# Transposes of k and x1 moved from TensorE to VectorE block transposes and SP transfers

## The chip, the cores and the metric

The kernel runs on one core of a Trainium2 chip. The metric is the device time of one execution in microseconds. A core has TensorE (matrix products and transposes through an identity matrix), VectorE and ScalarE (elementwise work, both read PSUM), GpSimd (POOL) and SyncE (SP), which here only issues DMA transfers. Every engine works through its own queue in order; semaphores order the engines among each other.

## The reference

Two layers on 4096 tokens (8 sequences of 512) with 256 features, all in float32:

```
q1, k1 = rotary(x @ Wq), rotary(x @ Wk)        # 4 heads of 64
v      = x @ Wv                                # 4 heads of 128
o      = chunked retention(q1 / 8, k1, v)      # per head: decayed causal scores and a state S (64 x 128)
o      = rmsnorm(o, gn_weight) * silu(x @ Wg)
x1     = layernorm(x + o @ Wo)
h      = silu(x1 @ w_gate.T / 127) * (x1 @ w_up.T / 127)     # 768 wide, integer weights
out    = layernorm(x1 + h @ w_down.T / 127)
```

## The kernel before

The tokens are cut into 32 tiles (NT) of 128 rows. The kernel is a software pipeline in which slot s works on several tiles at once: the projections of tile s, the scores and the state of tile s - 1, the output of the heads of tile s - 2, the product with Wo of tile s - 3, and the FFN of tiles further back. Most products are made of two or three passes over float32 operands split into a high part (fp32r) and a remainder, so that each operand exists as a "hi" and a "lo" tile. Each engine's order of work is written out by hand, in one block of code for each engine; slots 9 (PACKED) to 31 follow `packed_slot`, and a `drain` follows them. The state is kept in halves of 64 rows from tile 8 (CHUNKED) on.

TensorE's packed slot is, in order: `down` (tile s - 7), the gate and up products of block s - 1 (parts 0 and 1, b_ffn), `turn_y` of tile s - 3, `keys_and_queries` (k of tile s, and queries already turned), part 2 of the block, `attention_out` of tile s - 3, `heads` (recall, scores of tile s - 1, state update, output of tile s - 2), `project` for v and g (L545), `turn_x1` (L711) and `turn_qk` (L558). The last product of `attention_out` (L527, b_rows<-wo,yT) carries the waits of `heads_ready`, so the queue stands still there until everything that `heads` reads is in place. `keys_and_queries`, `attention_out`, `down` and the gate and up products all run through the helper line L527 and are told apart by their tiles.

How k gets to the scores: VectorE multiplies k by cosines and sines (`packed_rotate_k`, L1574, L1577) and adds them in `sum_k` (L1531), which writes qk[:, s % 2, 256:512] and raises `rotated`. TensorE's `turn_qk` at the end of the slot transposes the two 128x128 blocks into PSUM (b_turn) and raises `qkT_done`. ScalarE's `keep_qk` (L1097) copies them to qkT[:, 2:4] at the start of the next slot and raises `qkT_kept`, for which `heads_ready` waits. The scores read qkT; the state update reads qk as it is.

How x1 gets to the FFN: VectorE's `norm_1` (L1620) writes x1 of tile s - 3 late in slot s (into x1 or x1_late, a part of wf_int; `x1_of`). TensorE's `turn_x1` transposes its two 128x128 blocks into b_ffn. ScalarE's `split_x1T` (L1148) at the start of slot s + 1 casts them to x1T_hi, VectorE's `split_x1T` (L1668) subtracts to x1T_lo and raises `x1T_split`. A gate and up block works on a pair of tiles: `gate_up_block`, part 0, waits for the split of the tiles up to s - 2 - 1.

In `packed_slot` VectorE's order is: split_x1T, norm_2 (L1633), gated_output (L1728), residual_2 (L1758), hidden 0 and 1 (L1608), split_y (L1677), packed_rotate_k and _q, stats_2 (L1766), hidden 2, moments_2, residual_1 (L1740, L1742), moments_1, add_first_half (L1706, L1708), turned_sines (L1585), add_second_half (L1716), norm_1, sum_k, add_q (L1594), mask (L1652). ScalarE's is: split_x1T, gate_v, split_xT, keep_qk, gate 0 and 1 (L1199), split_y (L1174), split_h 0 and 1 (L1210), gate 2, turn_q (L1103, L1104), split_h 2, mean_squares (L1186), copy_v (L1137).

SP's slot issues in an even slot the load of xT (L425) and of x (L429, after residual_1 of tile s - 3), and in every slot the store of a tile of the output (L482, after norm_2). It has nothing else to do after the start.

Of the kernel before, what the change touches and what calls it, by code (L numbers as in the profile page):

```python
# [55 lines left out]
PACKED = NATURAL + 1  # L56
CHUNKED = PACKED - 1


# [23 lines left out]
def build_block(nc, xT, x, w_proj, w_o, gn, w_ffn, rope, rope_by_row, out):  # L83
# [5 lines left out]
    with ExitStack() as ctx:  # L89
# [6 lines left out]
        def sem(name):  # L96
# [85 lines left out]
            for c, n, rings in ((0, 1, 2), (1, 1, 2), (2, 1, 2), (3, 2, 4)))  # L182

        def ffn_part(c):
            return slice(c * NF // NFP, (c + 1) * NF // NFP)
# [42 lines left out]
        q_first_done, q_first_copied, q_first_turned = sem("q_first_done"), sem("q_first_copied"), sem("q_first_turned")  # L228
        qkT_done, qkT_kept = sem("qkT_done"), sem("qkT_kept")
        v_copied, g_gated = sem("v_copied"), sem("g_gated")  # L230
        scores_done, masked = sem("scores_done"), sem("masked")
# [75 lines left out]
        def ffn_before(b, j):  # L307

            if (b, j) in LAST_FFN_BANKS:
                same = [x for x, place in LAST_FFN_BANKS.items() if place == ffn_at(b, j)]  # L310
                i = same.index((b, j))
                if i > 0:
                    return same[i - 1]
                return (NT - 2, 1) if ffn_at(b, j) == (3 * (NT - 2) + 1) % 2 else (NT - 2, 2)
            return (b, 0) if j == 2 else (b - 1, j + 1)

        def packed_rows(s, k):
# [105 lines left out]
        def _(sp):  # L423
# [34 lines left out]
            def slot(s, q, t):  # L458
# [17 lines left out]
                if exists(n):  # L476
# [4 lines left out]
                    else:  # L481
                        sp.dma_start(out[bass.ds(n * P, P), :], x2_of(n, tn % 2)).then_inc(stored[tn % 2], 16)  # L482

            def drain():

                for s in range(NT, LAST):
                    slot(s, s // TS, s % TS)
                for r in range(2):
                    sp.wait_ge(stored[r], 16 * (NT // 2))
                sp.wait_ge(last_stored, 16)  # L490

            for s in range(NT):
                slot(s, s // TS, s % TS)
            drain()


        @block.tensor
        def _(pe):
# [195 lines left out]
            def turn_x1(s, q, t):  # L694

                n, tn = s - X1T_LAG, back(q, t, X1T_LAG)[1]
                if exists(n):
                    pe.wait_ge(x1_ready, n + 1)
                    if isinstance(s, int) and s >= NT:
                        pe.wait_ge(y_ready, NT - 1)  # L700
                        pe.wait_ge(masked, NT)
                        pe.wait_ge(x1T_split, n)
                    elif ffn_slot(s - 1):
                        pe.wait_ge(h_ready[1], s - FFN_LAG)
                        if s >= PACKED and t > 0:
                            pe.wait_ge(next_kept, nexts_to(s - 1))
                    else:
                        pe.wait_ge(y_ready, 2)
                    dst = x1_bank(s, t)
                    for k in range(KD):  # L710
                        mm = pe.transpose(dst[:, k * P:(k + 1) * P], x1_of(n)[:, k * P:(k + 1) * P], ident[:])  # L711
                    mm.then_inc(x1T_done, 1)
# [34 lines left out]
            def turn_y(s, q, t):  # L747

                n = s - 2
                if exists(n):  # L750
                    pe.wait_ge(y_ready, n + 1)
                    if n + 3 > PACKED:
                        pe.wait_ge(qkT_kept, min(n + 3, NT))
                        pe.wait_ge(yT_split, n)
                    else:
                        wait_bank(s, 0, turn_stages)
# [9 lines left out]
            def heads_ready(s):  # L766

                n, m = s - 1, s - 2
                pe.wait_ge(qkT_kept, n + 1)
                pe.wait_ge(q_rotated, s - 8 if n % 2 else s - 7)  # L770
# [91 lines left out]
            def gate_up_block(s, q, t, j, wide, last_waits=None):  # L862
# [5 lines left out]
                if j == 0 or s >= NT - 1:  # L868

                    behind = 2 if s < NT - 1 or t % 2 == 0 or s == NT - 1 and dst is x1_bank(s, t) else 3  # L870
                    pe.wait_ge(x1T_split, s - behind)

                if s < PACKED:
                    if j == 0 and t > 0:
                        pe.wait_ge(state_half, halves_to(s - 1, q, t - 1))
                bb, jb = ffn_before(s, j)
                if ffn_slot(bb):
# [102 lines left out]
            def packed_slot(s, wide):  # L980
# [16 lines left out]
                turn_x1(s, q, t)  # L997
                turn_qk(s, q, t)

# [80 lines left out]
        def _(act):  # L1080
# [8 lines left out]
            def keep_qk(s, q, t):  # L1089

                n = s - 1
                if exists(n):
                    act.wait_ge(qkT_done, n + 1)
                    if exists(n - 1):
# [44 lines left out]
            def split_x1T(s, q, t):  # L1139

                n = s - X1T_LAG
                if exists(n):
                    ring, at = ((t - 3) // 2) % 2, ((t - 3) % 2) * P
                    act.wait_ge(x1T_done, n + 1)

                    if exists(n - 4):
                        act.wait_ge(ffn_done[2], n - 2 if (t - 3) % 2 == 0 else n - 3)
                    act.copy(x1T_hi[:, ring, :, at:at + P],  # L1148
                             x1_bank(s, t)[:, 0:KD * P].rearrange("p (k n) -> p k n", k=KD)).then_inc(x1T_high, 1)

# [109 lines left out]
            def packed_slot(s):  # L1260
# [5 lines left out]
                else:  # L1266
                    split_x1T(*at(s - 4, X1T_LAG))
                    gate_v(*at(s, -1))
# [8 lines left out]
                split_h(b, tb, 0)  # L1277
                split_h(b, tb, 1)
                gate(b, tb, 2)
                turn_q(s, q, t, 0)  # L1280
# [139 lines left out]
        def _(dve):  # L1420
# [97 lines left out]
            def sum_k(s, q, t):  # L1518

                if exists(s):  # L1520
                    if has_q(s, t):
                        dve.wait_ge(k_parts, s - NATURAL + 1)
                    else:
                        dve.wait_ge(rot_parts, s + 1)
                    dve.wait_ge(qkT_done, s - 1)
                    if s - 2 >= CHUNKED:
# [3 lines left out]
                    for e, sign in ((0, ALU.subtract), (1, ALU.add)):  # L1530
                        last = dve.tensor_tensor(halves(qk[:, t % 2, 256:512])[:, :, e],  # L1531
                                                 halves(rot_c[:, 256:512])[:, :, e],
                                                 halves(rot_s[:, 256:512])[:, :, e], sign)
                    last.then_inc(rotated, 1)

            def finish_q(s, q, t):
# [73 lines left out]
            def norm_1(s, q, t):  # L1610

                n, tn = s - X1T_LAG, back(q, t, X1T_LAG)[1]
                if exists(n):
# [3 lines left out]
                    if exists(n - 8):  # L1617
                        dve.wait_ge(z2_ready, n - 7)
                        dve.wait_ge(x1T_done, n - 7)
                    dve.tensor_scalar(x1_of(n), z1[:], mv1[:, 0:1], rs1[:, 0:1], ALU.subtract,  # L1620
                                      ALU.mult).then_inc(x1_ready, 1)

            def norm_2(s, q, t):
# [38 lines left out]
            def split_x1T(s, q, t):  # L1662

                n = s - X1T_LAG
                if exists(n):
                    ring, at = ((t - 3) // 2) % 2, ((t - 3) % 2) * P
                    dve.wait_ge(x1T_high, n + 1)
                    dve.tensor_tensor(x1T_lo[:, ring, :, at:at + P],  # L1668
                                      x1_bank(s, t)[:, 0:KD * P].rearrange("p (k n) -> p k n", k=KD),
                                      x1T_hi[:, ring, :, at:at + P].bitcast(F32), ALU.subtract).then_inc(x1T_split, 1)  # L1670
# [138 lines left out]
            def packed_slot(s):  # L1809

                q, t = s // TS, s % TS
                b, tb = s - 1, (s - 1) % TS
                if s > PACKED:
                    split_x1T(*at(s - 4, X1T_LAG))
# [11 lines left out]
                packed_rotate_k(s, q, t)  # L1826
                packed_rotate_q(s, q, t)
                stats_2(*at(s - 7, DOWN_LAG))
                hidden(b, tb, 2)
# [6 lines left out]
                add_second_half(s - 1)  # L1836
                norm_1(*at(s - 3, X1T_LAG))
                sum_k(s, q, t)
                add_q(s, q, t)
                mask(*at(s - 1, 1))  # L1840
# [349 lines left out]
```

## Time and profile before

| | us |
|---|---|
| median of 3 runs | 423.6 (423.06 to 423.93) |
| the profiled execution, its own time | 423.2 |
| its span, from the first to the last instruction | 421.5 |
| TensorE busy in it | 412.1 (98%) |
| VectorE busy | 313.2 (74%) |
| ScalarE busy | 268.2 (64%) |
| GpSimd busy | 183.2 (43%) |

The granted TensorE clock is 0.999 of full speed on average. TensorE's products overlap in its pipeline: one is listed with 0.28 us, while the next starts 0.115 us after it, so starts are to be compared, not durations. SP issues 84 transfers in the whole kernel, 4 in two packed slots.

### The profile page before, as it was taken

To read this page: it belongs to the slowest core of one execution; us is meant where nothing else is said; L and a number is where in the kernel's file an instruction comes from. 1 tells how busy PE (TensorE), PEld (TensorE's weight loads), DVE (VectorE), ACT (ScalarE), POOL (GpSimd) and SP (SyncE) were. 2 spreads that over 40 slices of the span, in tenths; PEclk is the share of its full clock that TensorE was granted. 3 is DMA by queue.
4 is the path that set the end of the run, shared out by engine and by line. 5 is a ranking of instruction groups with operands and counts; after the bars stand their busy time and mean duration, and the time that the engine had idled before them with its cause. 6 is when DMAs were issued, how large, how long until landed. Compare 5 with 4: busy or idle time off the path is not lost.

```text
span 421.5 us, 12747 instructions
## 1 busy us (share of the span) xinstructions
PE 412.1 (98%) x4698; PEld 394.4 (94%) x4698; DVE 313.2 (74%) x912; ACT 268.2 (64%) x812; POOL 183.2 (43%) x330
## 2 busy tenths in 40 slices
PE   8999999998999999999999999999999999999994
PEld 6899999998999999999999999999999999998994
DVE  4999776677777777867777867777777777784975
ACT  6678655577666766766766766666666666654551
POOL 2532344355344455334355344445443434442654
PEclk9999999999999999999999999999999999999999
DMA  8931010101020201102020110201110010100001
GB/s 284 360 131 52 0 51 2 53 14 39 12 68 2 76 2 40 39 2 77 2 55 25 40 40 2 76 2 40 39 26 29 2 51 2 40 14 15 15 25 55
DMA packets 14352, 19.99 MB, mean 47 GB/s; under 512 B 1488, under 2 KB 9808, under 8 KB 14288
## 3 DMA queue, kind: packets, MB, share of 16 engines
q1 hardware_dynamic: 14144, 19.08, 14.1%
q8 instruction: 40, 0.66, 0.6%
q14 instruction: 24, 0.20, 0.2%
q10 hardware_dynamic: 144, 0.07, 0.1%
HBM read 14.94 MB, written 4.19 MB: 45 GB/s over the span
## 4 chain that ended last, share of the span: by engine, by line
PE 94%; DVE 2%; DMA 1%; issue 1%; POOL 1%; ACT 0%; SPq 0%; POOLq 0%; DVEq 0%; ACTq 0%
PE b_rows L527 30%; PE b_rows L545 20%; PE b_ffn L527 20%; PE b_turn L763 3%; PE b_head L793 3%; PE b_head L801 3%; PE b_turn L558 2%; PE b_state L820 2%; PE b_ffn L711 2%; PE b_head L722 2%; PE b_head L814 1%; PE b_rows L541 1%; DMA wf_int<-in_w_proj 1%; PE b_head L689 1%; PE b_head L685 1%
## 5 line engine op out<-in xcount | busy, mean ns | idle before, releaser
L2032 POOL TENSOR_TENSOR h_lo<-wf_int,h_hi 128x256 fp32r<-128x256 f32 x96 | 70.0, 742 | 121.7 <-ACT h_hi L1210 121.7
L527 PE MATMUL b_ffn<-x1T_hi,wf_hi 128*128 128x256 f32 x384 | 92.0, 279 | 0.1
L527 PE MATMUL b_ffn<-x1T_lo,wf_hi 128*128 128x256 f32 x384 | 91.5, 278 | 0.0
L1199 ACT ACTIVATE wf_int<-b_ffn 128x256 f32<-128x256 f32 x96 | 36.9, 384 | 59.5 <-PE b_ffn L527 59.4
L527 PEld LDWEIGHTS b_ffn<-x1T_hi,wf_hi 128*128 128x128 f32 x384 | 72.2, 188 | 0.6 <-DVE x1T_lo L1668 0.2
L527 PEld LDWEIGHTS b_ffn<-x1T_lo,wf_hi 128*128 128x128 f32 x384 | 72.2, 188 | 0.0
L545 PE MATMUL b_rows<-wp_hi,xT_hi 128*128 128x256 f32 x230 | 66.4, 289 | 1.2 <-issue 1.2
L545 PE MATMUL b_rows<-wp_hi,xT_lo 128*128 128x256 f32 x244 | 66.5, 277 | 0.0
L545 PE MATMUL b_rows<-wp_lo,xT_hi 128*128 128x256 f32 x230 | 63.8, 277 | 0.0
L1608 DVE TENSOR_TENSOR wf_int<-b_ffn,wf_int 128x256 f32<-128x256 f32 x96 | 40.2, 419 | 26.3 <-ACT wf_int L1199 25.7
L1186 ACT ACTIVATE sq<-b_head 128x128 f32<-128x128 f32 x120 | 33.3, 278 | 28.7 <-PE b_head L801 19.6
L527 PE MATMUL b_rows<-wf_hi,h_hi 128*128 128x256 f32 x192 | 48.4, 291 | 0.5 <-ACT g_sb L1158 0.2
L545 PEld LDWEIGHTS b_rows<-wp_hi,xT_hi 128*128 128x128 f32 x230 | 43.1, 188 | 5.7 <-issue 5.2
L527 PE MATMUL b_rows<-wf_hi,h_lo 128*128 128x256 f32 x192 | 45.7, 277 | 0.0
L545 PEld LDWEIGHTS b_rows<-wp_hi,xT_lo 128*128 128x128 f32 x244 | 45.4, 188 | 0.3
L545 PEld LDWEIGHTS b_rows<-wp_lo,xT_hi 128*128 128x128 f32 x230 | 43.3, 188 | 0.2
L1210 ACT CAST h_hi<-wf_int 128x256 fp32r<-128x256 f32 x96 | 36.7, 407 | 8.1 <-DVE wf_int L1608 7.5
L527 PEld LDWEIGHTS b_rows<-wf_hi,h_hi 128*128 128x128 f32 x192 | 36.1, 188 | 1.1 <-POOL h_lo L2032 0.6
L2052 POOL TENSOR_TENSOR rs<-ve,half_neg 128x1 f32<-128x1 f32 x63 | 34.3, 544 | 4.9
L2050 POOL TENSOR_TENSOR ve<-mv,eps 128x1 f32<-128x1 f32 x63 | 12.2, 194 | 55.6 <-DVE mv L1749 31.3
L527 PE MATMUL b_rows<-wo_hi,yT_hi 128*128 128x256 f32 x128 | 36.3, 284 | 0.0
L527 PEld LDWEIGHTS b_rows<-wf_hi,h_lo 128*128 128x128 f32 x192 | 36.2, 188 | 0.0
(191 smaller groups left out, 1166.5 us busy)
## 6 DMA issues: line engine op xcount, KB each, us to landing
xT_raw<-in_xT SPq DMA_DIRECT2D x16, 256.0 KB, 2.8
x_sb<-in_x SPq DMA_DIRECT2D x16, 256.0 KB, 3.0
out<-wf_int SPq DMA_DIRECT2D x30, 128.0 KB, 1.8
wf_int<-in_w_ffn SPq DMA_DIRECT2D x6, 384.0 KB, 6.7
wf_int<-in_w_proj SPq DMA_DIRECT2D x6, 256.0 KB, 4.7
rope_sb<-in_rope SPq DMA_DIRECT2D x4, 256.0 KB, 5.7
rope_q<-in_rope_by_row SPq DMA_DIRECT2D x2, 512.0 KB, 9.5
wo_raw<-in_w_o SPq DMA_DIRECT2D x1, 512.0 KB, 6.4
```

Source lines behind the costliest of these rows:

```text
L527: mm = pe.matmul(dst, a, b, start=(i == 0 and j == 0 and not begun), stop=(i == n - 1 and j == len(passes) - 1 and not more), skip_group_c ...
L545: mm = pe.matmul(dst[:, cols], a, b[:, cols], start=c == 0 and i == 0, stop=i == n - 1, skip_group_check=True)
L763: mm = pe.transpose(dst, y[:, h * P:(h + 1) * P], ident[:])
L793: mm = pe.matmul(o_of(m, h)[out_rows(h, a)], queries(m, h, a), kept[half(h), h // 2], start=h < 2, stop=False, skip_group_check=True)
L801: mm = pe.matmul(o_of(m, h)[out_rows(h, a)], attn[half(a), h, 0:CHUNK], v_sb[half(a), m % 2, h * DV:(h + 1) * DV], start=False, stop=True, ...
L1186: act.activation(sq[:], o_of(n, h), ACT.Square, scale=float(DV) ** -0.5, accum_out=ms[:, tn % 2, h:h + 1]).then_inc(squared, 1)
L1199: act.activation(act_g[:, u], b_ffn[u][:, 0:256], ACT.Silu, scale=SCALE).then_inc(silu_done[j], 1)
L1210: act.copy(h_hi[:, ((t - FFN_LAG) // 2) % 2, hb], h_full[:, u]).then_inc(h_high[j], 1)
L1608: dve.tensor_tensor(h_full[:, u], b_ffn[u][:, 256:512], act_g[:, u], ALU.mult).then_inc(h_ready[j], 1)
L2032: pool.tensor_tensor(h_lo[:, ring, hb], h_full[:, u], h_hi[:, ring, hb].bitcast(F32), ALU.subtract).then_inc(h_split[j], 1)
L2050: pool.tensor_tensor(ve, mv[:, 1:2], eps[:, 0:1], ALU.add).then_inc(var, 1)
L2052: pool.tensor_tensor(rs, ve, half_neg[:, 0:1], ALU.pow).then_inc(rstd, 1)
```

## The change

The k of tiles 9 to 30 and the x1 of the even tiles 8 to 26 no longer go through TensorE. VectorE transposes the 32x32 blocks inside each group of 32 partitions (a quadrant), one instruction for the 128x256 tile, into a buffer of its own (`k_blocks`, `x1_blocks`, both in a part of wf_int that is free by then). SP then copies the blocks to the quadrant that they belong to: sixteen transfers for k (each 32 partitions x 2 blocks x 32 elements, with runs of 128 bytes) straight into qkT, and sixteen for x1 into `x1T_raw`. ScalarE's copy of k goes; ScalarE and VectorE split x1 from `x1T_raw` in place of PSUM, and do so later in their slot for the moved tiles. `heads_ready` waits for the transfers of k, `k_moved`, in place of `qkT_kept`. The diff without the new semaphores' and buffers' declarations:

```diff
+        def moved(n):
+            return PACKED <= n < NT - 1
+        def moves(n):
+            return 16 * (P // BLOCK) ** 2 * (n - PACKED + 1)
+        def turned_before(n):
+            return min(n, PACKED)
+        def moved_x1(n):
+            return n % 2 == 0 and CHUNKED <= n < NT - 5
+        def x1_moves(n):
+            return 16 * (P // BLOCK) ** 2 * ((n - CHUNKED) // 2 + 1)
...
         # SP
+            def move_k(n):
+                blocks = k_blocks.rearrange("p (b j c) -> p b j c", b=2, c=BLOCK)
+                sp.wait_ge(k_blocked, n - PACKED + 1)
+                sp.wait_ge(scores_done, n)
+                for i in range(P // BLOCK):
+                    src = slice(i * BLOCK, (i + 1) * BLOCK)
+                    for j in range(P // BLOCK):
+                        sp.dma_start(qkT[j * BLOCK:(j + 1) * BLOCK, 2:4, src], blocks[src, :, j, :]).then_inc(k_moved, 16)
+            def move_x1(n):
+                blocks = x1_blocks.rearrange("p (k j c) -> p k j c", k=KD, c=BLOCK)
+                sp.wait_ge(x1_blocked, (n - CHUNKED) // 2 + 1)
+                sp.wait_ge(x1T_split, n - 1)
+                for i in range(P // BLOCK):
+                    src = slice(i * BLOCK, (i + 1) * BLOCK)
+                    for j in range(P // BLOCK):
+                        sp.dma_start(x1T_raw[j * BLOCK:(j + 1) * BLOCK, :, src], blocks[src, :, j, :]).then_inc(x1_moved, 16)
...
             for s in range(NT):
                 slot(s, s // TS, s % TS)
+                if s >= PACKED and moved_x1(s - 3):
+                    move_x1(s - 3)
+                if moved(s):
+                    move_k(s)
             drain()
...
         # TensorE: turn_x1, turn_y, heads_ready, gate_up_block, packed_slot
-                if exists(n):
+                if exists(n) and not moved_x1(n):
                     pe.wait_ge(x1_ready, n + 1)
...
-                        pe.wait_ge(qkT_kept, min(n + 3, NT))
+                        if n + 3 == PACKED + 1 or n + 3 >= NT:
+                            pe.wait_ge(qkT_kept, turned_before(n + 3) + (1 if n + 3 >= NT else 0))
                         pe.wait_ge(yT_split, n)
...
-                pe.wait_ge(qkT_kept, n + 1)
+                if moved(n):
+                    pe.wait_ge(k_moved, moves(n))
+                else:
+                    pe.wait_ge(qkT_kept, turned_before(n) + 1)
...
                     behind = 2 if s < NT - 1 or t % 2 == 0 or s == NT - 1 and dst is x1_bank(s, t) else 3
+                    behind = 3 if moved_x1(s - 3) else behind
                     pe.wait_ge(x1T_split, s - behind)
...
+                elif j == 0 and s < NT and t > 0:
+                    pe.wait_ge(next_kept, nexts_to(s - 1))
...
                 turn_x1(s, q, t)
-                turn_qk(s, q, t)
+                if not moved(s):
+                    turn_qk(s, q, t)
...
         # ScalarE: keep_qk, split_x1T, packed_slot
-                if exists(n):
-                    act.wait_ge(qkT_done, n + 1)
+                if exists(n) and not moved(n):
+                    act.wait_ge(qkT_done, turned_before(n) + 1)
...
-                    act.wait_ge(x1T_done, n + 1)
+                    if moved_x1(n):
+                        act.wait_ge(x1_moved, x1_moves(n))
+                    else:
+                        act.wait_ge(x1T_done, x1_turns(n) + 1)
...
-                    split_x1T(*at(s - 4, X1T_LAG))
+                    if not moved_x1(s - 4):
+                        split_x1T(*at(s - 4, X1T_LAG))
...
                 split_h(b, tb, 1)
+                if moved_x1(s - 4):
+                    split_x1T(*at(s - 4, X1T_LAG))
                 gate(b, tb, 2)
...
         # VectorE
+            def block_k(n):
+                dve.wait_ge(rotated, n + 1)
+                if n > PACKED:
+                    dve.wait_ge(k_moved, moves(n - 1))
+                dve.transpose(k_blocks, qk[:, n % 2, 256:512]).then_inc(k_blocked, 1)
+            def block_x1(n):
+                if n > CHUNKED:
+                    dve.wait_ge(x1_moved, x1_moves(n - 2))
+                dve.wait_ge(x1_ready, n + 1)
+                dve.transpose(x1_blocks, x1_of(n)).then_inc(x1_blocked, 1)
...
-                if s > PACKED:
+                if s > PACKED and not moved_x1(s - 4):
                     split_x1T(*at(s - 4, X1T_LAG))
...
                 packed_rotate_q(s, q, t)
+                if moved_x1(s - 4):
+                    split_x1T(*at(s - 4, X1T_LAG))
                 stats_2(*at(s - 7, DOWN_LAG))
...
                 norm_1(*at(s - 3, X1T_LAG))
+                if moved_x1(s - 3):
+                    block_x1(s - 3)
                 sum_k(s, q, t)
+                if moved(s):
+                    block_k(s)
                 add_q(s, q, t)
```

## Rows read from the trace of the kernel before

**Rows 1.** The page: busy time by engine, and the chain that ended last.

```profile
PE 412.1 (98%) x4698; PEld 394.4 (94%) x4698; DVE 313.2 (74%) x912; ACT 268.2 (64%) x812; POOL 183.2 (43%) x330
...
PE 94%; DVE 2%; DMA 1%; issue 1%; POOL 1%; ACT 0%; SPq 0%; POOLq 0%; DVEq 0%; ACTq 0%
```

**Rows 2.** Timeline of TensorE (start us, duration us, line, what, count) around two heads.

```profile
213.21 0.28 PE L527 MATMUL b_rows<-wo_hi,yT_lo 128*128 128x256 f32 x1
...
214.47 0.27 PE L820 MATMUL b_ffn<-v_sb,qk 64*64 64x128 f32 x1
...
225.65 0.28 PE L527 MATMUL b_rows<-wo_hi,yT_lo 128*128 128x256 f32 x1
```

**Rows 3.** Timeline of SP's issues over two steady slots.

```profile
213.97 0.39 SPq L429 DMA_DIRECT2D x_sb<-in_x  x1
214.41 5.49 SPq L482 DMA_DIRECT2D out<-wf_int  x2
...
238.89 0.39 SPq L429 DMA_DIRECT2D x_sb<-in_x  x1
```

**Rows 4.** Timeline of VectorE behind the first of these heads.

```profile
214.80 0.42 DVE L1708 TENSOR_TENSOR state_mid<-b_state,states 128x256 f32<-128x256 f32 x1 [0.18 <-PE b_ffn L820]
215.15 0.41 DVE L1585 TENSOR_TENSOR rot_s<-q_turn,rope_q 128x256 f32<-128x256 f32 x1
215.81 0.56 DVE L1620 TENSOR_SCALAR wf_int<-z,mv,rs 128x256 f32<-128x256 f32 x1
216.29 0.48 DVE L1531 TENSOR_TENSOR qk<-rot_c,rot_s 128x128 f32<-128x128 f32 x2
```

**Rows 5.** Timeline of TensorE around the transposes of x1 and k.

```profile
205.51 0.38 PE L711 MATMUL b_ffn<-ident,wf_int 128*128 128x128 f32 x2
205.72 0.38 PE L558 MATMUL b_turn<-ident,qk 128*128 128x128 f32 x2
205.86 0.37 PE L527 MATMUL b_rows<-wf_hi,h_hi 128*128 128x256 f32 x1
206.06 0.28 PE L527 MATMUL b_rows<-wf_hi,h_lo 128*128 128x256 f32 x1
```

**Rows 6.** Timeline of SP at the start: issues that follow each other.

```profile
1.24 2.79 SPq L433 DMA_DIRECT2D wf_int<-in_w_proj  x6
4.08 0.43 SPq L439 DMA_DIRECT2D rope_sb<-in_rope  x1
...
6.21 0.48 SPq L443 DMA_DIRECT2D gn_sb<-in_gn  x1
6.73 0.46 SPq L429 DMA_DIRECT2D x_sb<-in_x  x1
```

**Rows 7.** Timeline of SP, an issue after a wait, and a longer one.

```profile
10.15 0.34 SPq L452 DMA_DIRECT2D wf_int<-in_w_ffn  x1
...
14.88 0.71 SPq L429 DMA_DIRECT2D x_sb<-in_x  x1
```

**Rows 8.** DMA: GB/s in 40 slices; issues (count, KB, median us to landing).

```profile
GB/s 284 360 131 52 0 51 2 53 14 39 12 68 2 76 2 40 39 2 77 2 55 25 40 40 2 76 2 40 39 26 29 2 51 2 40 14 15 15 25 55
...
out<-wf_int SPq DMA_DIRECT2D x30, 128.0 KB, 1.8
...
out<-v_sb SPq DMA_DIRECT2D x1, 128.0 KB, 2.5
```

**Rows 9.** Windows at the end (us, busy by engine, PEclk, DMA share, GB/s).

```profile
416.00:417.00 1.00, 0.25 (x3) 0.05 (x1) 0.87 (x4) 0.00 (x0) 0.61 (x2) 1.00 0.39 129
417.00:420.00 3.00, 0.00 (x0) 0.00 (x0) 1.39 (x6) 0.40 (x1) 0.67 (x2) 1.00 0.23 70
420.00:421.50 1.50, 0.00 (x0) 0.00 (x0) 0.00 (x0) 0.00 (x0) 0.00 (x0) 0.67 0.16 48
```

**Rows 10.** Timeline of ScalarE ahead of gate 2.

```profile
222.71 0.71 ACT L1210 CAST h_hi<-wf_int 128x256 fp32r<-128x256 f32 x2
224.55 0.39 ACT L1199 ACTIVATE wf_int<-b_ffn 128x256 f32<-128x256 f32 x1 [1.12 <-PE b_ffn L527]
```

More of the change, by code:

```diff
@@ L57 @@
 CHUNKED = PACKED - 1
+BLOCK = 32
 def rope_tables():
@@ L182, in build_block @@
             for c, n, rings in ((0, 1, 2), (1, 1, 2), (2, 1, 2), (3, 2, 4)))
+        k_blocks = wf_int[:, 5 * 512:5 * 512 + 256].bitcast(F32)
+        x1_blocks = wf_int[:, 5 * 512 + 256:6 * 512].bitcast(F32)
+        x1T_raw = wf_int[:, 6 * 512:6 * 512 + 256].bitcast(F32).rearrange("p (k n) -> p k n", k=KD)
         def ffn_part(c):
@@ L229, in build_block @@
         qkT_done, qkT_kept = sem("qkT_done"), sem("qkT_kept")
+        k_blocked, k_moved = sem("k_blocked"), sem("k_moved")
+        x1_blocked, x1_moved = sem("x1_blocked"), sem("x1_moved")
         v_copied, g_gated = sem("v_copied"), sem("g_gated")
@@ L315, in ffn_before, with x1_turns @@
             return (b, 0) if j == 2 else (b - 1, j + 1)
+        def moved(n):
[8 more added lines that the diff above has]
+            return 16 * (P // BLOCK) ** 2 * ((n - CHUNKED) // 2 + 1)
+        def x1_turns(n):
+            return sum(not moved_x1(i) for i in range(n))
         def packed_rows(s, k):
@@ L1143, in split_x1T @@
                     ring, at = ((t - 3) // 2) % 2, ((t - 3) % 2) * P
-                    act.wait_ge(x1T_done, n + 1)
+                    if moved_x1(n):
+                        act.wait_ge(x1_moved, x1_moves(n))
+                    else:
+                        act.wait_ge(x1T_done, x1_turns(n) + 1)
                     if exists(n - 4):
                         act.wait_ge(ffn_done[2], n - 2 if (t - 3) % 2 == 0 else n - 3)
-                    act.copy(x1T_hi[:, ring, :, at:at + P],
-                             x1_bank(s, t)[:, 0:KD * P].rearrange("p (k n) -> p k n", k=KD)).then_inc(x1T_high, 1)
+                    src = x1T_raw if moved_x1(n) else x1_bank(s, t)[:, 0:KD * P].rearrange("p (k n) -> p k n", k=KD)
+                    act.copy(x1T_hi[:, ring, :, at:at + P], src).then_inc(x1T_high, 1)
             def gate_v(s, q, t):
@@ L1524, in sum_k @@
                         dve.wait_ge(rot_parts, s + 1)
-                    dve.wait_ge(qkT_done, s - 1)
+                    if not moved(s - 2):
+                        dve.wait_ge(qkT_done, s - 1)
                     if s - 2 >= CHUNKED:
@@ L1618, in norm_1 @@
                         dve.wait_ge(z2_ready, n - 7)
-                        dve.wait_ge(x1T_done, n - 7)
+                        if not moved_x1(n - 8):
+                            dve.wait_ge(x1T_done, x1_turns(n - 8) + 1)
                     dve.tensor_scalar(x1_of(n), z1[:], mv1[:, 0:1], rs1[:, 0:1], ALU.subtract,
                                       ALU.mult).then_inc(x1_ready, 1)
+            def block_x1(n):
[3 more added lines that the diff above has]
+                dve.transpose(x1_blocks, x1_of(n)).then_inc(x1_blocked, 1)
             def norm_2(s, q, t):
@@ L1667, in split_x1T @@
                     dve.wait_ge(x1T_high, n + 1)
-                    dve.tensor_tensor(x1T_lo[:, ring, :, at:at + P],
-                                      x1_bank(s, t)[:, 0:KD * P].rearrange("p (k n) -> p k n", k=KD),
+                    src = x1T_raw if moved_x1(n) else x1_bank(s, t)[:, 0:KD * P].rearrange("p (k n) -> p k n", k=KD)
+                    dve.tensor_tensor(x1T_lo[:, ring, :, at:at + P], src,
                                       x1T_hi[:, ring, :, at:at + P].bitcast(F32), ALU.subtract).then_inc(x1T_split, 1)
```

## The prediction

> **What bounds the kernel now.** I read the page's busy shares and its chain of waits first: TensorE is busy for 98% of the span and carries 94% of the chain that ended last [rows 1]. So each TensorE instruction that goes is worth its time, and each new wait that ends late costs its time, because TensorE has no slack to give back. Then I laid the timelines of one steady slot side by side. TensorE starts the last product of attention_out at 213.21 and again at 225.65 [rows 2]. I call this instant h: it is where heads_ready holds the queue, ahead of heads. A slot is 12.44 us, and over two slots (the loads of x, 213.97 to 238.89) 24.92, so 12.46 each [rows 3]. VectorE in the same slot: norm_1 starts 215.81, sum_k's pair of additions ends at 216.77 [rows 4]. From h that is 3.56 us to the rotated k. TensorE turns it and ScalarE keeps it long before the next heads: now k has 12.46 - 3.56 = 8.9 us from rotation to use, and it needs a fraction.
>
> SP is the queue that the change loads. Now it issues 4 transfers in two slots, each in about 0.4 us, and waits for the rest of the 25 us [rows 3]. So the new transfers find an idle queue, and the question is how fast one instruction follows the other.
>
> **What is removed.** For 22 tiles two transposes of qk on TensorE, for 10 tiles two of x1. In the timeline the x1 pair starts at 205.51, the k pair at 205.72, the next product at 205.86 and the one behind it at 206.06 [rows 5]. The x1 pair takes 0.21. The k pair takes 0.14, and 0.08 more if the product after it gets back to the usual distance of about 0.12; I take 0.18. Were everything new hidden, the kernel would win 22 x 0.18 + 10 x 0.21 = 6.1 us. ScalarE also loses its 22 copies to qkT; it is not on the chain [rows 1], so I count them as nothing.
>
> **What is added on VectorE.** One block transpose of 128x256 per k and one per x1. The trace of before has none. Other 128x256 operations of VectorE last 0.41 to 0.56, and two start 0.35 apart [rows 4]. Below: 0.35. Above: twice the costliest of these rows, 1.1, since a reordering need not stream as an addition does. I take 0.4, the nearest rows (same size, same memory). It sits on the new path: rotated, block, SP.
>
> **What is added on SP: the step that decides.** Each k is 16 transfers of 8 KB (32 partitions x 2 x 128 bytes), each x1 another 16, all on one queue. 22 x 16 + 10 x 16 = 512 issues. The price of one issue: at the start six loads of w_proj start at 1.24 and the next instruction at 4.08, (4.08 - 1.24) / 6 = 0.47 each; gn_sb to x_sb, 6.21 to 6.73, 0.52 [rows 6]. The load after a wait is shorter: 0.34, and with the 0.04 between two instructions 0.38 [rows 7]. Size hardly shows: gn_sb is 0.5 KB (128 partitions x 4 bytes) and takes 0.48 against 0.43 of rope's 256 KB, and x_sb, with two runs per partition, takes 0.39 [rows 3, 6]. So 0.47 per issue in a run, bounds 0.38 and 0.52. Nothing excludes a smaller price with 32 partitions in place of 128, but no row shows it; it is a rival below.
>
> Landing after the issue: median 1.8 us for out (from SBUF, 128 KB), 2.5 for one of the last stores of the same size [rows 8]. I take 1.8; below, 1.8 less the 0.4 that 128 KB spends moving at 360 GB/s, the fastest slice [rows 8], so 1.4; above 2.5. The packets themselves are few: 64 a transfer over 16 DMA engines.
>
> The Trainium skill (DMA: Bandwidth & Descriptors, "Anatomy of one DMA") puts the sequencer's dispatch at about 50 ns and nearly all of the 2 us into the write receipt, and under "Issuing engines are not separate DMA queues" it calls the time to initiate "usually small relative to the DMA itself". This trace disagrees for small transfers: 0.47 us between issues. By that rule the changed kernel would win its 6.1 us. The same page's rules say that transfers under 64 KB are mostly overhead and should be merged, which speaks against the change.
>
> **The sum.** With k moved, a slot's step from h to the next h can't be shorter than the chain h, rotated, block, 16 issues, landing.
> - A slot without x1 moves (12 of the 22: s = 9, 10 and the even ones 12 to 30): 3.56 + 0.4 + 0.05 for the hand-over = 4.0; the sixteenth issue starts 15 x 0.47 = 7.05 later; landing 1.8; 0.1 until TensorE goes on: 12.95 us. TensorE's own work in that slot is 12.46 - 0.18 = 12.28, so the stall is 0.7 and the step grows by 0.5.
> - A slot with x1 moves (10: s = 11, 13, ... 29): the code puts move_x1 before move_k on SP. norm_1 ends 216.37, 3.16 after h; the block transpose of x1 0.4; 3.6 and 0.05: issues start at 3.65. 32 issues follow, the last starts 31 x 0.47 = 14.57 later; 1.8 and 0.1: 20.1 us. TensorE's work is 12.1, so it stands still for 8 us.
>
> The 22 steps are now 22 x 12.46 = 274.1. After: 10 x 20.1 + 12 x 12.95 = 356.4, that is +82.3.
>
> **The clock.** In this trace TensorE has no more work from about 416.25 on; the granted clock is full in 417 to 420 and 0.67 on average in 420 to 421.5 [rows 9], so it has gone from 2.4 to 1.2 GHz in there. The ten stalls of 8 us are longer than this idle end of 5. So I expect 1.2 GHz when TensorE goes on after each of them. The step after it begins slow: from h to the state update is about 1.3 us of TensorE (213.21 to 214.5, before add_first_half at 214.80 [rows 2, 4]), which at half speed is 1.1 longer, on the chain to rotated. Ten times 1.1 is +11; nothing, if the clock comes back at once; 2 per stall, if the slow stretch lasts into the projections. The Trainium skill (TensorE: Matmul & The Clock Gate, "Rules for kernel authors") also says that long gaps between bursts send the array back to half rate; by it the sum is 11 higher than without the clock, as above.
>
> **Other waits, and why they are at nothing.** split_x1T of ScalarE now waits for x1's transfers in the next slot: they land at 3.65 + 7.05 + 1.8 = 12.5 after h, while ScalarE comes to it about 10.2 after h (the casts to h_hi end at 223.42 [rows 10]). gate(2), split_h(2), VectorE's hidden(2) are queued behind it and are 2.3 us late. TensorE is by then held at heads until 20.1, which covers it; were that cover gone, it would cost up to 2 us in each of 10 slots. The out, x and xT transfers stand in front of or behind the runs of 16 on SP: in even slots x and out are issued at h + 0.76 and h + 1.20, ahead of the k moves; the out of an odd slot is ready at about 219.5, where the two stores of 214.41 to 219.90 end [rows 3] and waits up to 5 us for the queue, and VectorE asks for its buffer two slots later. The xT load keeps more than one slot of lead. The changed wait of gate_up_block 0 (an x1 tile further back) only makes room.
>
> Sum: 423.2 (the profiled execution; the median of the runs is 423.6, so no correction) + 82 + 11 = 516.
>
> **The rivals.**
> - *The issue is cheap for small transfers, and all is hidden.* For: the issues in the trace are all of 128 partitions, none has 32. The Trainium skill's sentences above (DMA: Bandwidth & Descriptors) speak for it too. Against: gn_sb's 0.48 for 0.5 KB [rows 6]. The point from which it decides: an x1 slot fits into 12.1 when 5.55 + 31 i < 12.1, i = 0.21 us. Then TensorE wins its transposes: 423.2 - 6.1 = 417. This is the one on the other side. 9%.
> - *Issues between 0.21 and 0.38*: k slots hidden (4.0 + 15 x 0.3 + 1.9 = 10.4), x1 slots at 5.55 + 31 x 0.3 = 14.9: 10 x 14.9 + 12 x 12.28 - 274.1 = +22, 445. 6%.
> - *SP backs up.* One issue took 0.71 while the start's loads filled the DMA engines [rows 7]. If a run of 16 were priced so, i = 0.65: x1 slots 25.7, k slots 15.65, +171 and the clock: 605. Against: those were hundreds of KB each, these are 8. 6%.
> - *The clock stays full*: 505. Inside my forecast's range.
> - The change does what it says: no tile keeps its old path beside the new one, so that rival I leave out.
>
> **How the numbers follow.** The forecast with its own bounds holds 79%: from i = 0.38, landing 1.4 and a full clock (x1 step 16.9, k step at the floor 12.28: +42, 466) to i = 0.52 with landing 2.1 and the clock (x1 22.0, k 14.0, +114 and +13: 550). Range 455 to 552. What can be told from no change is about 0.2%. Faster takes the first rival, 9%; same 1%, the border between the first two; slower the remaining 90%.
>
> **What would show it.** Right: on SP, runs of 16 and 32 issues at about 0.47; TensorE's steps alternating between about 13 to 14 and 20 us, its idle time of 7 to 8 us in ten places, released by the DMA of qkT; the granted clock below 1 behind these. Wrong: SP's 16 issues done in under 4 us; the idle time elsewhere, as on x1T; a block transpose above 1 us (each 0.1 more is 0.1 in each of the 22 steps, so +2).

## The result

| | before | changed |
|---|---|---|
| median of 4 runs each, us | 423.8 | 621.7 (620.9 to 622.3) |
| ratio, with its 95% interval | 1 | 1.467 (1.464 to 1.470) |
| span of the profiled execution, us | 421.5 | 619.8 |
| granted TensorE clock, mean | 0.999 | 0.862 |

The forecast was slower, 516 us, range 455 to 552. The direction and the mechanism came out, the size did not: +198 us in place of +93.

The page of the changed kernel first: busy times, granted clock in 40 slices, and the chain that ended last by engine and by its first lines. They answer to [rows 1].

```profile
PE 445.6 (72%) x4634; PEld 420.6 (68%) x4634; DVE 326.4 (53%) x944; ACT 259.7 (42%) x790; POOL 182.0 (29%) x330
...
PEclk9999999888598787795995896886968869859999
...
SPq 49%; PE 29%; DVE 8%; DMA 7%; issue 6%; ACT 1%; POOL 0%; POOLq 0%; DVEq 0%; ACTq 0%
SPq L524 33%; SPq L534 16%; PE b_rows L583 7%; DMA qkT<-wf_int 6%; PE b_ffn L583 4%; PE b_rows L601 3%; PE b_head L853 3%; PE b_state L880 2%; PE b_head L874 1%; DVE wf_int L1699 1%; PE b_head L778 1%; PE b_rows L597 1%; DVE qk L1602 1%; DVE states L1802 1%; DVE wf_int L1612 1%
```

TensorE was 94% of the chain and is 29% now. SP's queue, which was on it with 0%, is 49%: L524 is move_k, L534 move_x1. Next, the waits (who waited for whom, us in total, times, longest). TensorE's last product ahead of heads is L583, b_rows<-wo_hi,yT_lo.

```profile
PE b_rows L583 <- DMA qkT<-wf_int: 164.2, 22, 14.4
...
ACT x1T_hi L1216 <- DMA wf_int<-wf_int: 52.8, 10, 6.5
```

All 22 steps have the new wait, and ScalarE stands ten times before x1. One pair of slots on SP's timeline, and the two ends of the same steps on TensorE's:

```profile
312.76 10.96 SPq L534 DMA_DIRECT2D wf_int<-wf_int  x16
323.82 10.17 SPq L524 DMA_DIRECT2D qkT<-wf_int  x16
334.03 0.58 SPq L457 DMA_DIRECT2D xT_raw<-in_xT  x1
336.28 0.40 SPq L461 DMA_DIRECT2D x_sb<-in_x  x1
336.73 0.46 SPq L514 DMA_DIRECT2D out<-wf_int  x1
```

```profile
307.78 0.39 PE L583 MATMUL b_rows<-wo_hi,yT_lo 128*128 128x256 f32 x1 [2.44 <-DMA qkT<-wf_int]
...
335.21 0.58 PE L583 MATMUL b_rows<-wo_hi,yT_lo 128*128 128x256 f32 x1 [13.56 <-DMA qkT<-wf_int]
...
352.62 0.38 PE L583 MATMUL b_rows<-wo_hi,yT_lo 128*128 128x256 f32 x1 [2.88 <-DMA qkT<-wf_int]
```

The step with x1 moves lasts 27.4 us (307.78 to 335.21), the one without 17.4; both were 12.46. Over the whole trace the ten steps with x1 moves last 25.5 to 27.5 us, 26.7 on average, and the others 16.4 to 17.7. In the long one SP starts 4.98 us after h and then issues without a pause for 21.2 us; TensorE goes on about 1.2 us after the last issue has ended. The price of an issue is in the two lines' own rows (duration ns min/median/max); the page gives 1.8 us from issue to landing for both, as forecast:

```profile
L524 SPq DMA_DIRECT2D qkT<-wf_int x352: 585/597/1644, 106.0 to 569.7; - x176
...
L534 SPq DMA_DIRECT2D wf_int<-wf_int x160: 585/597/1457, 140.0 to 541.3; - x160
```

With the 0.04 us between two instructions that is 0.64 per issue, where I had 0.47. The block transposes took what they were thought to take, 0.45 us for 0.4 (group by line: count, busy us, mean ns):

```profile
L1612 DVE STREAM_TRANSPOSE wf_int<-qk 128x256 f32<-128x256 f32 x22 | 9.8, 446 | 0.8
```

And the clock (windows; the figure behind the bracketed counts is the granted clock):

```profile
307.00:310.00 3.00, 2.22 (x56) 2.09 (x59) 1.03 (x3) 0.00 (x0) 0.53 (x2) 0.79 0.18 52
...
316.00:324.00 8.00, 5.65 (x49) 5.44 (x48) 2.92 (x8) 1.97 (x5) 1.43 (x2) 1.00 0.09 14
324.00:334.00 10.00, 0.00 (x0) 0.00 (x0) 1.17 (x4) 2.54 (x7) 0.73 (x2) 0.59 0.08 12
334.00:336.00 2.00, 0.79 (x7) 0.57 (x11) 0.18 (x1) 0.00 (x0) 0.00 (x0) 0.50 0.30 67
336.00:340.00 4.00, 4.00 (x63) 3.67 (x60) 2.65 (x9) 0.89 (x5) 1.42 (x3) 0.57 0.46 135
```

TensorE works until 321.6, the clock falls in the idle stretch, and heads starts at half speed.

**Where the 105 us between forecast and result lie.** From the first k run's first issue (105.96) to the last one's (559.10) there are 21 steps and 453.1 us: 314.0 from the first to the last issue of each step, and 139.1 between the last issue of a step and the first of the next (landing, heads, rotation, block). My formula gives 10 x 14.57 + 11 x 7.05 = 223.3 for the first and 131 with the clock for the second. So 91 of the missing us are issue time: 475 intervals x (0.639 - 0.47) = 80, and 11 for the rest, most of it in 15 issues of the 512 that took over 0.7 us, up to 1.64. The gaps are 8 over. The remaining 6 or so are in the first and the last step and I have not assigned them.

### The profile page after: what moved, and what is told of

Same layout as the page of the kernel before. It is cut to its first block, busy times and chain, and to the rows that moved or that the text cites. A ratio compares the mean times of both kernels' runs of the same rounds, so it can differ in the third digit from the quotient of the medians.

```text
span 619.8 us, 13149 instructions
## 1 busy us (share of the span) xinstructions
PE 445.6 (72%) x4634; PEld 420.6 (68%) x4634; DVE 326.4 (53%) x944; ACT 259.7 (42%) x790; POOL 182.0 (29%) x330
## 4 chain that ended last, share of the span: by engine, by line
SPq 49%; PE 29%; DVE 8%; DMA 7%; issue 6%; ACT 1%; POOL 0%; POOLq 0%; DVEq 0%; ACTq 0%
SPq L524 33%; SPq L534 16%; PE b_rows L583 7%; DMA qkT<-wf_int 6%; PE b_ffn L583 4%; PE b_rows L601 3%; PE b_head L853 3%; PE b_state L880 2%; PE b_head L874 1%; DVE wf_int L1699 1%; PE b_head L778 1%; PE b_rows L597 1%; DVE qk L1602 1%; DVE states L1802 1%; DVE wf_int L1612 1%
## 5 line engine op out<-in xcount | busy, mean ns | idle before, releaser
L583 PE MATMUL b_rows<-wo_hi,yT_lo 128*128 128x256 f32 x128 | 40.8, 318 | 164.2 <-DMA qkT<-wf_int 164.2
L583 PEld LDWEIGHTS b_rows<-wo_hi,yT_lo 128*128 128x128 f32 x128 | 25.4, 198 | 168.6 <-DMA qkT<-wf_int 168.6
L583 PE MATMUL b_ffn<-x1T_hi,wf_hi 128*128 128x256 f32 x384 | 92.3, 280 | 0.1
L583 PE MATMUL b_ffn<-x1T_lo,wf_hi 128*128 128x256 f32 x384 | 91.8, 278 | 0.0
L1826 DVE TENSOR_TENSOR z<-b_rows,x_sb 128x256 f32<-128x256 f32 x32 | 13.5, 423 | 144.5 <-PE b_rows L583 144.4
L583 PEld LDWEIGHTS b_ffn<-x1T_hi,wf_hi 128*128 128x128 f32 x384 | 72.3, 188 | 0.6 <-DVE x1T_lo L1755 0.2
L583 PEld LDWEIGHTS b_ffn<-x1T_lo,wf_hi 128*128 128x128 f32 x384 | 72.2, 188 | 0.0
L601 PE MATMUL b_rows<-wp_hi,xT_hi 128*128 128x256 f32 x230 | 70.9, 308 | 1.2 <-issue 1.2
L601 PE MATMUL b_rows<-wp_hi,xT_lo 128*128 128x256 f32 x244 | 68.9, 287 | 0.0
L601 PE MATMUL b_rows<-wp_lo,xT_hi 128*128 128x256 f32 x230 | 66.8, 291 | 0.0
L601 PEld LDWEIGHTS b_rows<-wp_hi,xT_hi 128*128 128x128 f32 x230 | 46.9, 204 | 7.9 <-issue 7.4
L601 PEld LDWEIGHTS b_rows<-wp_hi,xT_lo 128*128 128x128 f32 x244 | 48.5, 201 | 0.3
L583 PE MATMUL b_rows<-wf_hi,h_hi 128*128 128x256 f32 x192 | 47.7, 287 | 0.5 <-ACT g_sb L1225 0.2
L601 PEld LDWEIGHTS b_rows<-wp_lo,xT_hi 128*128 128x128 f32 x230 | 47.2, 205 | 0.2
L583 PE MATMUL b_rows<-wf_hi,h_lo 128*128 128x256 f32 x192 | 46.0, 278 | 0.0
L583 PEld LDWEIGHTS b_rows<-wf_hi,h_hi 128*128 128x128 f32 x192 | 36.2, 189 | 1.1 <-POOL h_lo L2124 0.6
```

The lines of the kernel that those rows point to most:

```text
L583: mm = pe.matmul(dst, a, b, start=(i == 0 and j == 0 and not begun), stop=(i == n - 1 and j == len(passes) - 1 and not more), skip_group_c ...
L601: mm = pe.matmul(dst[:, cols], a, b[:, cols], start=c == 0 and i == 0, stop=i == n - 1, skip_group_check=True)
L1826: dve.tensor_tensor(z1[:], wo_bank(s, t)[:, 0:D], x_sb[:, tn, :], ALU.add).then_inc(z1_ready, 1)
```

## The experiments

Theory A: the number of issues on SP times their price sets the steps. Its rivals: B, the many small packets burden the DMA engines or the landing; C, x1's way through ScalarE is the larger harm; and the clock. "h" is as in the prediction. Each run is beside the kernel before on the same chip, 422.5 to 423.7 us; a time without an interval is that of one execution.

**Only k moved** (`moved_x1` returns False):

```diff
-            return n % 2 == 0 and CHUNKED <= n < NT - 5
+            return False
```

> Only k goes through SP (22 runs of 16 transfers); x1 stays on TensorE. Theory A (SP's price per issue decides, 0.64 us here): every one of the 22 steps is h, rotated and blocked (4.0 us, 5.0 at the lower clock) + 15 x 0.64 + 1.9 = 15.5 to 16.5 us in place of 12.46, so +67 to +89: 491 to 513 us. Theory B (the landing or the DMA engines suffer from 512 small transfers, the price per issue only mirrors that): with a third fewer transfers the issue falls towards 0.47 and the steps towards 13, about 436 to 445. Theory C (the x1 part is the larger harm by itself, through ScalarE): under 440.

521.0 us, +98.5. Steps alternate no more; they are 15.6 to 17.7 us, 16.8 on average. The issue price is still 0.64 with a third fewer transfers in the kernel, which is against B (how many follow each other at once is the same here, and is tested by the prices below). The time is 8 us above the upper end: 18 of the 352 issues took over 0.7 us, which adds 12 us in all that I had not priced.

**Only x1 moved** (`moved` returns False, the waits on qkT as before):

```diff
-            return PACKED <= n < NT - 1
+            return False
```

> Only x1 of the ten even tiles goes through SP; k stays on TensorE. Theory A: its 16 transfers start 3.65 us after h and land at 3.65 + 9.6 + 1.8 = 15 us, ScalarE stands before split_x1T from about 10.2 on, so it comes to gate 2 and to the turned queries about 4 us late, and TensorE's projection of v, which waits for these, stalls about 3 us in each of ten slots: 423.8 + 30 - 2 = about 452. If the cover holds (TensorE does not wait for any of it): 421.7. The sum of the effects of e1 and e2 should fall well short of or near the whole +198, of which the ten steps with 32 issues carry most.

476.3 us, +53.9, or 5.4 in each of ten slots; expected 3. ScalarE waits and TensorE is held in v's projection (L601), not at heads; the wait before it is listed as issue:

```profile
ACT x1T_hi L1215 <- DMA wf_int<-wf_int: 58.6, 10, 6.5
...
PE b_rows L601 <- issue: 40.7, 11, 4.6
```

So x1 costs by itself too, through gate 2 and the turned queries behind it. The prediction had this cost at nothing for its cover, and up to 2 us without it; it is 5.4. The granted clock was 0.965 in this run, and how much of the 5.4 is the clock is not separated. The two parts add up to 152; the other 46 of the 198 come with both together, in the ten slots in which 32 issues stand on one queue.

**The price of an issue by itself.** The kernel before, with 8 further transfers in each of slots 9 to 30 that only SP waits for.

```diff
+            def price(s):
+                sp.wait_ge(priced, 16 * 8 * (s - PACKED))
+                for d in range(8):
+                    if (s - PACKED) % 11 == 0:
+                        sp.dma_start(wf[:, d, :], rs[:, d, :]).then_inc(priced, 16)
...
+                    if (s - PACKED) % 11 == 7:
+                        sp.dma_start(wf[0:32, d, :], x[0:32, :]).then_inc(priced, 16)
```

> The kernel before, with 8 further transfers on SP in each of slots 9 to 30 into a scratch part, nothing waits for them but SP: eleven shapes, two slots each. Time unchanged, 423 to 425, as SP is idle. Prices per issue (start to start): theory A1 (it is the second dimension with short runs): 32 partitions x 2 runs of 128 B 0.64, 128 partitions x 2 runs of 128 B the same or more, one run of 1 KB 0.47 whatever the partitions. Theory A2 (it is that both ends lie in SBUF): all SBUF to SBUF shapes 0.64, all from HBM 0.47. Theory A3 (it is fewer than 128 partitions, as work is dealt out to 16 rings): the 32-partition shapes 0.64, the 128-partition ones 0.47. Theory B (back-pressure of many small packets): more packets cost more, 128 x 2 runs dearest.

> The kernel before with runs of 8 further transfers of eleven shapes on SP, as in the first price run. If the price is set by whether both ends are in SBUF or an end has two runs: one run to or from HBM 0.42 to 0.47 at any size and number of partitions; two runs with an end in HBM 0.64 on whichever side the second run is; SBUF to SBUF of 16 partitions 0.63. If it is the second dimension on the HBM side alone: two runs in SBUF only 0.46. Time 423 to 425.

424.0 and 424.6 us: they lie in SP's idle time. Some of the runs of 8, from both:

```profile
115.48 5.05 SPq L506 DMA_DIRECT2D wf_int<-rope_sb  x8
121.89 5.71 SPq L508 DMA_DIRECT2D wf_int<-rope_sb  x8
147.49 5.01 SPq L512 DMA_DIRECT2D wf_int<-rope_sb  x8
196.09 5.17 SPq L520 DMA_DIRECT2D wf_int<-in_x  x8
```

```profile
122.89 3.63 SPq L509 DMA_DIRECT2D wf_int<-in_x  x8
147.07 3.59 SPq L513 DMA_DIRECT2D wf_int<-in_x  x8
165.49 5.12 SPq L515 DMA_DIRECT2D spill<-rope_sb  x8
197.07 5.17 SPq L521 DMA_DIRECT2D spill<-in_x  x8
```

The medians from start to start, in us, by partitions x bytes of one run:

| ends | one run per row | two runs on both sides |
|---|---|---|
| SBUF to SBUF | 0.63 (32 x 1 KB, L506), 0.63 (32 x 128 B, L512; 16 x 128 B), 0.64 (128 x 1 KB; 128 x 128 B) | 0.64 (32, as the kernel's, L508; 32 that stay in their quadrant), 0.65 (64), 0.67 (128) |
| HBM to SBUF | 0.46 (32 x 1 KB), 0.46 (32 x 128 B, L513), 0.48 (128 x 1 KB) | 0.65 (32, L520), 0.65 (128), 0.64 (32, four runs) |
| SBUF to HBM | 0.46 (32 x 1 KB), 0.49 (128 x 1 KB) | 0.64 (32, L515) |
| HBM to HBM | 0.63 (32 x 1 KB, L521) | |

Two runs on one side only: 0.47 (L509, two in SBUF, 32 rows) and 0.51 (two in HBM, 128 rows). Where SBUF to SBUF and HBM to SBUF transfers took turns, a pair cost 1.2, more than the 1.10 of one of each kind by itself. So neither bytes nor partitions set the price, nor the number of packets (B falls), nor the move between quadrants; A3 falls too, and A1 and A2 are each true in part. It is 0.46 to 0.51 when exactly one end is in HBM and one side is a single run, and 0.63 to 0.67 when both ends are in the same memory or both sides have two runs. The kernel's transfers are both. The second run's expectation of 0.64 for two runs on either side alone was wrong. Why these kinds are dearer no run shows. All the rows that I had priced from [rows 6, 7] are of the cheap kind.

**Products without use in the stalls.** In the changed kernel 50 of them ahead of k's wait in x1 slots, 10 in the others; later, with k alone moved, 16 in each step:

```diff
                 if moved(n):
+                    for _ in range(50 if moved_x1(n - 3) else 10):
+                        pe.matmul(b_state[:, 256:256 + P], ones[:], ones[:], start=True, stop=True, skip_group_check=True)
                     pe.wait_ge(k_moved, moves(n))
```

> The changed kernel with products without use in TensorE's stalls: 50 of 128 columns (10.7 us at full clock) before the wait for k in the ten slots with x1 moves, 10 (2.1 us) in the others; they fit into the stalls. If the low clock costs what the changed trace suggests (issues start 5.0 us after h in place of 3.65 or 4.0, 22 times): 597, with a granted clock near 1. If the clock costs nothing: 621. If the products overrun the stalls: above 621.

> Only k moved (16 issues each), with 16 products without use (3.4 us at full clock) in TensorE's stall of each of the 22 slots, which was 4.6 us on average. In the run without them 13 of 21 steps began at the lower clock and their k moves started about 1 us later after h (7.0 against 6.0 us after the last issue). If the clock is what delays them: the granted clock near 1 and 521 - 13 = 508, within 4 for the long issues that come at random. If not: 521.

The first took 629.7 us and tells nothing of the clock's price: its clock still fell at the end of the long stalls (0.53 in the 3 us after the one below), and it had 26 long issues for 15, which is what the 8 us are.

```profile
286.00:292.00 6.00, 6.00 (x54) 5.81 (x53) 0.05 (x1) 1.04 (x3) 0.73 (x2) 1.00 0.09 13
292.00:295.00 3.00, 0.26 (x2) 0.19 (x1) 0.00 (x0) 0.00 (x0) 0.00 (x0) 1.00 0.20 26
295.00:298.00 3.00, 3.00 (x57) 2.79 (x56) 1.58 (x5) 0.00 (x0) 1.43 (x3) 0.53 0.59 166
```

The second is cleaner: clock 0.994 in place of 0.93, as many long issues (19 for 18), 513.6 in place of 521.0. (The wait before k was 65.0 us over 22 steps in the run without products, so 3.0 on average and not 4.6; the 16 products fill it nearly whole.) The time from a step's last issue to the next one's first was 6.0 to 6.2 us in 6 of 21 steps without the products and 6.4 to 7.2 in the others, 139.8 in all; with them it is 6.0 to 6.3 in 19 steps, and 130.1 in all. So the low clock costs 0.4 to 1.2 us in a step that it touches, 9.7 in all. Of these 7.4 are seen in the time. The run with products is 1.8 us later already when it issues the load of x at 83.70 (81.88 without), before the first of the products, and the stretch behind its last issue is 2.0 us longer; its issues are 1.5 shorter in all. I had expected 508.

**Four wide transfers in place of sixteen:**

```diff
-                for i in range(P // BLOCK):
-                    src = slice(i * BLOCK, (i + 1) * BLOCK)
-                    for j in range(P // BLOCK):
-                        sp.dma_start(qkT[j * BLOCK:(j + 1) * BLOCK, 2:4, src], blocks[src, :, j, :]).then_inc(k_moved, 16)
+                for j in range(P // BLOCK):
+                    sp.dma_start(qkT[:, 2:4, j * BLOCK:(j + 1) * BLOCK], blocks[:, :, j, :]).then_inc(k_moved, 16)
```

> The changed kernel with 4 transfers of 128 partitions for each k and x1 (the same bytes, the same two runs of 128 B per partition) in place of 16 of 32 partitions: the blocks stay in their quadrant, so this leaves out the move between quadrants; block transposes, waits and order are the same. Theory A (number of issues x 0.64 on SP): an x1 slot's chain is 3.9 + 7 x 0.65 + 1.9 = 10.4 us, a k slot's 4.4 + 3 x 0.65 + 1.9 = 8.3, both under TensorE's own 12.1 to 12.3; all is hidden and the transposes are won: 417 to 419. Theory B (the bytes or the packets of 128 B burden the path): as many packets as before, so still far above 423. Theory D (the block transposes or the moved splits themselves cost): a remainder above 423.

416.5 us. This kernel leaves out the move between quadrants, so the scores and the FFN read blocks in the wrong order; it serves for its time alone. With a quarter of the issues, and the same bytes, data packets, block transposes and waits, 205 us are gone. The queue's packets (number, MB, share), the changed kernel first, and then the chain that ended last in this one:

```profile
q1 hardware_dynamic: 55104, 23.30, 14.2%
```

```profile
q1 hardware_dynamic: 48960, 23.28, 21.2%
...
PE 94%; DVE 2%; issue 1%; DMA 1%; POOL 1%; ACT 0%; SPq 0%; POOLq 0%; DVEq 0%; ACTq 0%
```

The 6,144 packets less are 16 for each of the 384 issues less. TensorE carries the chain again as before the change. That shows theory A, and it shows the gain that the change was after: 423.6 - 416.5 = 7, forecast 6.1.

**The k moves ahead of the x1 moves** (the two calls in SP's loop swapped):

> The changed kernel with the k moves ahead of the x1 moves on SP. Theory A with a shared queue: heads then waits only for 16 issues (about 16 us), but x1 lands at 4.2 + 31 x 0.64 + 1.9 = 26 us after h, and ScalarE stands before split_x1T until then with gate 2 and the turned queries behind it, for which v's projection and through VectorE the next rotated k wait: the pair of slots stays at about 43 us, 610 to 625 in all, the idle time moving from k's transfers to x1's. If only the wait for k mattered: ten steps fall from 27 to 16.5, about 515.

633.9 us, 9 above the upper end of 625. The idle time moves, as expected: from the wait for qkT to ScalarE's for x1 and, through it, to v's projection.

```profile
ACT x1T_hi L1216 <- DMA wf_int<-wf_int: 166.1, 10, 17.4
...
PE b_rows L601 <- issue: 96.7, 11, 11.2
PEld b_rows L583 <- DMA qkT<-wf_int: 75.7, 22, 4.9
```

Neither order helps: a pair of slots has 48 such issues, 48 x 0.64 = 30.7 us of SP's time, and the pair took 24.9 us before. So at this price the moves can't be hidden by any order on one queue.

**By way of HBM.** One store writes the blocked tile to HBM, and four loads, each for 32 partitions, read the blocks back in the order that is wanted: they do what sixteen transfers did. For k:

```diff
+                sp.dma_start(spill[n % 2], k_blocks).then_inc(k_spilled, 16)
...
+                sp.wait_ge(k_spilled, 16 * (n - PACKED + 1))
+                sp.wait_ge(scores_done, n)
+                for b in range(4):
+                    sp.dma_start(qkT[b * BLOCK:(b + 1) * BLOCK, 2:4, :].rearrange("p b (i c) -> p b i c", c=BLOCK),
+                                 spill[n % 2].rearrange("(i p) (b j c) -> j p b i c", p=BLOCK, b=2, c=BLOCK)[b]).then_inc(k_moved, 16)
```

> Only k moved, and by way of HBM: one store of the blocked tile (128 partitions x 1 KB) and, once it has landed, four loads of 32 partitions that put the blocks into their quadrants: 5 issues in place of 16. Theory A: 4.2 + store 2.0 to land + 3 x 0.64 + landing 2.4 to 3 = 10.5 to 11.1 us after h, under TensorE's 12.3: hidden, and 22 pairs of transposes are won: 423.8 - 4 = about 420. If the store's landing plus the loads' with runs of 128 B take above 6 us: steps above 12.5 and no gain.

> k and x1 moved by way of HBM: 10 issues in an x1 slot, x1's loads ahead of k's. Theory A: x1 stored at 3.9, landed about 5.9; eight loads of 0.64 start from there, the last at 10.4, landing 2.4: 12.8 + 0.1 against TensorE's 12.07, so these ten steps are 12.9 in place of 12.46, the twelve others 12.28: 423.8 + 4.4 - 2.2 = about 426; with a longer landing up to 432.

> k and x1 by way of HBM as in the run with 10 issues in an x1 slot, but two of x1's four loads are issued by ScalarE ahead of gate 0. Theory A: SP's last k load then starts at 5.9 + 5 x 0.64 = 9.1 us, k lands by 11.4 to 11.6, under TensorE's 12.07: the stall of these ten slots goes, all 6.1 us of transposes are won: 417 to 418.5. The two issues hold ScalarE for 1.2 us ahead of gate 0; if that is not slack of ScalarE's, TensorE waits for it at the gate and up products, up to 0.8 us in ten slots: 425.

| | us | ratio (95%) |
|---|---|---|
| k alone, 5 issues | 419.8 | 0.991 (0.988 to 0.995) |
| k and x1, 10 issues in an x1 slot on SP | 425.6 | 1.005 (1.003 to 1.007) |
| the same, two of x1's loads issued by ScalarE | 417.9 | 0.987 (0.985 to 0.988) |

All three came out as the sum of issues and landings said. The two rows of SP are of the run with k alone and show k's path, 5 issues and 4.2 us where the sixteen took 10.2; a landing is 1.7 us for the store and 2.2 for the loads.

```profile
215.81 0.33 SPq L521 DMA_DIRECT2D spill<-wf_int  x1
217.52 2.54 SPq L528 DMA_DIRECT2D qkT<-spill  x4
```

In the second run TensorE again waits ten times, 8.4 us in all; two issues less on SP in a slot take that away, and ScalarE had the time for them. The last kernel beats the one before by 5.8 us, 1.3%.

## Why the prediction was wrong in size

- *What is removed*: 6.1 us forecast; the two kernels without the new stalls gained 5.8 and 7. Right.
- *The block transpose*, 0.4: 0.45. Right.
- *The price of an issue*: the term of the sum that was mis-sized. 0.47, bounds 0.38 to 0.52; it is 0.64. "Nothing excludes a smaller price with 32 partitions" shows the error: I bounded the price on the side of the size, which does not matter, and took all rows from transfers with one end in HBM. That both ends of the new ones are in SBUF, with two runs each, was in the diff, and no row of before has either. The price runs through 31 or 15 gaps of each step, so 0.17 us became 80 in 475 gaps. With 0.64 in place of 0.47 the prediction's own sum, clock included, gives 600.
- *Long issues*: 11 us that I had not in the sum. The opening had one of 0.71 [rows 7], which I took for a full queue. They come in slots with an idle DMA as well, and in the kernel before too (two stores of out took 1.34 and 1.61). What they go with can be read off the traces: the profile lists two DMA queues of kind "instruction", q8 and q14. The changed kernel has 39 packets on q8. From 20 us on, all 18 of this kernel's issues above 0.9 us have such a packet between 0.5 us before their start and their end, while 33 of all 570 issues do; over all 13 traces it is 159 of 165. The packets of q14 show no such tie. That a fetch of instructions holds the issue is the likely reading, but no run removed these packets. One case, three issues of which one takes 1.46, and the queue's packets from 445 to 446 us:

```profile
444.57 3.03 SPq L534 DMA_DIRECT2D wf_int<-wf_int  x3
```

```profile
q8 instruction: 1, 0.02, 8.6%
```

- *Landing*, 1.8: 1.8, exactly.
- *The steps*: x1 slots 26.7 on average (25.5 to 27.5) for 20.1, k slots 16.4 to 17.7 for 12.95 (14.05 behind a long stall). For the long one on show: 4.98 until SP starts, 31 x 0.64, 0.8 of long issues, 1.8 for the landing, 27.4.
- *The clock*, +11: at full clock the gaps are 5.7 (into an x1 run) and 6.0 (into a k run), so 10 x 5.7 + 11 x 6.0 = 123; they sum to 139. That is 16: 11 in the gaps into a k run, as forecast, and 5 or 6 in six of the ten gaps into an x1 run, because the clock fell in the k slots' stalls of 0.9 to 4.3 us too (0.79 in 307 to 310 us, around the stall that ends at 307.78). The Trainium skill's rule on idle gaps between bursts of products (TensorE: Matmul & The Clock Gate, "Why this matters for your kernels", the heading that the prediction meant) agrees: the clock fell in the stall of 13.6 us above.
- *The range*: it took 2.1 for the landing where the bound worked out before was 2.5. With 2.5 its upper end is 559, still far below.
- *Other waits at nothing*: under the cover of k's wait it held, but x1 alone costs 54.
- *The rivals*: "SP backs up", 0.65 and 605 us, has the number but not the reason: transfers of 4 KB in an otherwise idle queue cost 0.63. The rival on the other side, cheap issues, is false for the same rows. The 50 ns that the prediction set against 0.47 stand in a section of the Trainium skill on transfers issued by GpSimd (DMA: Bandwidth & Descriptors, "Anatomy of one DMA"); here SP issues, at 0.46 or more in a run, so they never bore on this kernel. The Trainium skill's advice to coalesce transfers under 64 KB (DMA: Bandwidth & Descriptors, "Rules for kernel authors") is borne out: the same bytes in a quarter of the issues, though without the move between quadrants, took 416.5 us.

## What to carry to other kernels

Count the DMA instructions of a queue before their bytes: here each held SP for 0.46 to 0.67 us whatever its size, so sixteen a slot cost 10.2 us of a 12.46 us slot. Price them from a row with the same kinds of memory at both ends and the same runs; where there is none, put the bound on that side and multiply by the count before you call the range narrow. Then hold the queue's whole load against the time it has: 48 issues of 0.64 us do not fit into two slots of 12.46. Here the block transposes cost VectorE only 0.45 us each, and what decided was how their blocks got to the other partitions: one store to HBM with four loads was a shorter way between partition groups than sixteen direct transfers.

## What the runs showed of the hardware that was not expected

- An issue of SP costs 0.46 to 0.51 us if exactly one end is in HBM and a side is one run, 0.63 to 0.67 if both ends are in SBUF or both in HBM, or both sides have two runs. 128 B or 1 KB, 16, 32 or 128 partitions differ by 0.04 at most within a kind. HBM to HBM was measured in one shape.
- The transfer right behind such a one is dearer too: out's store takes 0.58 right behind a run of SBUF to SBUF transfers of 32 partitions and 0.42 behind one from HBM; xT's load 0.58 and 0.42.
- 3 to 5 in 100 of the moves' issues took over 0.7 us, up to 1.8, and nearly all of those above 0.9 (159 of 165 in 13 traces) came together with a packet of the queue that the profile calls "instruction".
